# Linear attention of a macaron layer: the stage as a pipeline of 32 token tiles instead of a loop over batches

## What is computed

```python
    def step(carry, inp):
        mem, z = carry
        q_s, k_s, v_s = inp
        sq = jax.nn.elu(q_s) + 1.0
        att_mem = sq @ mem / (sq @ z)
        sk = jax.nn.elu(k_s) + 1.0
        mem = mem + jnp.einsum('bhlk,bhlv->bhkv', sk, v_s)
        z = z + sk.sum(axis=-2, keepdims=True).transpose(0, 1, 3, 2)
        att_dot = jax.nn.softmax(jnp.einsum('bhik,bhjk->bhij', q_s, k_s) * scale, axis=-1)
        att = att_dot @ v_s
        att = gate * att_mem + (1.0 - gate) * att
        return ((mem, z), att)
```

## Time and profile before

| what | value |
|---|---|
| time, median of 3 executions | 2392.57 us (2383.55, 2392.57, 2393.95) |
| the profiled execution | 2382.67 us, its span 2381.0 us |
| busy over the span: PE, DVE, ACT, POOL | 80%, 62%, 39%, 23% |
| attention stage, 844.4 to 1470.8 us | 626.4 us: PE 509.0, DVE 375.9, ACT 191.8, POOL 66.7 us busy |
| TensorE's mean granted clock, whole span and this stage | 0.90 and 0.86 of full speed |
| before it (feed-forward 1), behind it (feed-forward 2 and the last sum) | 844.4 and 910.2 us |

### The profile page before, as it was taken

One profiled execution on the slowest core, in us unless ns is written; L12 is line 12 of the kernel. 1 busy time (PEld: TensorE's weight loads), 2 busy tenths in 40 slices (PEclk: granted clock), 3 DMA queues, 4 the chain that ended last, 5 costly groups with the idle time before them and its releaser, 6 DMA issues. The chain is left out here.

```text
span 2381.0 us, 41513 instructions
## 1 busy us (share of the span) xinstructions
PE 1916.0 (80%) x12512; PEld 1065.6 (45%) x12513; DVE 1488.0 (62%) x3530; ACT 935.8 (39%) x1694; POOL 553.3 (23%) x640
## 2 busy tenths in 40 slices
PE   1899999998499958887888884599999998499940
PEld 1433333332299925565555663223333332189930
DVE  1678888884345437656666653487888886345533
ACT  0156666667222223332333321036666666322200
POOL 2222333311322231111001000222233331222246
PEclk9899999999699978888988986679999999799975
DMA  8336333320122231111011003335333330022245
GB/s 186 62 56 130 65 65 62 58 45 11 53 73 73 70 121 36 54 54 53 12 45 54 28 19 67 81 65 128 66 69 57 63 59 12 27 79 73 72 131 180
DMA packets 163076, 161.68 MB, mean 68 GB/s; under 512 B 20620, under 2 KB 153484, under 8 KB 162572
## 3 DMA queue, kind: packets, MB, share of 16 engines
q1 hardware_dynamic: 122048, 107.34, 19.7%
q10 hardware_dynamic: 30636, 27.21, 4.2%
q0 software_dynamic: 10240, 25.18, 3.7%
HBM read 90.80 MB, written 62.39 MB: 64 GB/s over the span
## 5 line engine op out<-in xcount | busy, mean ns | idle before, releaser
L576 DVE TENSOR_REDUCE f_M<-bank 128x1 f32<-128x512 f32 x1024 | 673.8, 685 | 194.0 <-PE bank L846 184.1
L486 ACT ACTIVATE f_PT<-bank 128x512 f32<-128x512 f32 x1024 | 573.0, 596 | 296.8 <-PE bank L863 292.2
L846 PE MATMUL bank<-f_KS,f_QS 96*128 96x512 bf16 x1024 | 403.8, 400 | 75.1 <-DVE f_M L576 39.1
L863 PE MATMUL bank<-f_QS,f_KS 99*128 99x512 bf16 x1024 | 394.8, 390 | 45.4 <-ACT f_PT L486 31.3
L863 PEld LDWEIGHTS bank<-f_QS,f_KS 99*128 99x128 bf16 x1024 | 99.9, 99 | 423.0 <-ACT f_PT L486 304.9
L873 PE MATMUL bank<-f_PT,f_V 128*32 128x512 f32 x2048 | 273.2, 607 | 0.0
L846 PEld LDWEIGHTS bank<-f_KS,f_QS 96*128 96x128 bf16 x1024 | 100.8, 99 | 204.8 <-DVE f_M L576 137.0
L1107 PE MATMUL bank<-f_room,f1m_gT 128*128 x568 | 136.2, 383 | 0.1
L1107 PE MATMUL bank<-f_room,f2m_gT 128*128 x568 | 135.3, 381 | 0.1
L415 POOL DMA_INDIRECT routed_rows<-f_AO,f_rows_i x128 | 124.7, 974 | 42.0 <-issue 42.0
L1107 PEld LDWEIGHTS bank<-f_room,f1m_gT 128*128 128x128 f32 x568 | 103.6, 193 | 11.8 <-issue 0.5
(11 more groups left out here) (257 smaller groups left out, 3027.4 us busy)
## 6 DMA issues: line engine op xcount, KB each, us to landing
f_QS<-q_parts SPq DMA_DIRECT2D x192, 64.0 KB
f_KS<-k_parts SPq DMA_DIRECT2D x168, 64.0 KB
expert_rows<-f1m_y ACTq DMA_DIRECT2D x71, 128.0 KB, 1.7
expert_rows<-f2m_y ACTq DMA_DIRECT2D x71, 128.0 KB, 1.7
xr<-f_xr SPq DMA_DIRECT2D x16, 512.0 KB, 3.0
f_room<-in_L_ffn_w SPq DMA_DIRECT2D x2, 4096.0 KB, 22.4
q_parts<-f_q SPq DMA_DIRECT2D x16, 384.0 KB, 2.5
k_parts<-f_k SPq DMA_DIRECT2D x16, 384.0 KB, 2.5
```

The source lines that it names most:

```text
L486: act.activation(PT[:, i % 8, :], SCE[i % 2][:, :], ACT.Exp).then_inc(probs_ready, 1)
L576: dve.tensor_reduce(M[:, t, h:h + 1], SCM[(a * SC + i) % 3][:, :], AX.X, ALU.max).then_inc(scm_drained, 1)
L846: pe.matmul(SCM[(a * SC + i) % 3][:, :], QS[par][0:K_MAX, h, t * P:(t + 1) * P], KS[par][0:K_MAX, h, :], start=True, stop=True).then_inc(s ...
L863: pe.matmul(SCE[i % 2][:, :], KS[par][0:K_EXP, h, t * P:(t + 1) * P], QS[par][0:K_EXP, h, :], start=True, stop=True).then_inc(sce_filled, 1)
```

## The change

It rewrites `attention_pass` and nothing else of weight. No arithmetic of the reference is left out.

- **One pipeline.** `SLOTS` becomes a list of 37 pairs (b, t), all written out, without a hardware loop: four slots that only prepare batch 0 (b = -1), 32 slots for the 32 tiles, and one behind them. Slot (b, t) holds score, recall, probabilities and from_memory of its tile g, and weigh, add_up, turn_out, project_out and put_out of tile g - 1.
- **Items.** `PLACES` gives the items of batch b + 1 to four places A to D in each of the four slots, k before q (`qk` 0 to 3 are now k). The last one, `mem` 6, falls into place A of the next batch's first slot. `sk` 0 waits for the four k features only, each `mem` item for its own v and sk, and `recall` for the memory of its own tile (`drained["mem"]` of 2t + 1) instead of the whole batch.
- **Banks.** Scores and recall share banks 0 and 1 (`SA`), so `recall` waits for `s_ready` of its tile and `score` for `am_read` of the tile before. `LB` is two banks, 2 and 3; `OB` is bank 4 and holds only `turn_out` and `project_out`. The ring has three banks, 5 to 7.
- **The sum.** `add_up` is (AM - L) * gate + L, three operations (two of them read PSUM) in place of gate * AM, omg * L and their sum (one of them reads PSUM). All three now stand between `weigh` and `turn_out`.
- **x** stays on chip in four buffers; x1, its store and its reload are gone, and `put_out` adds in place. Preparing batch b + 2 is cut into four parts, one for each slot. The steps for `gate` come behind the normalisation of batch 0.

```diff
+    PLACES = [{"A": [("hsT", 0), ("hsT", 1)], "B": [("qk", 0)], "C": [("qk", 1)], "D": [("qk", 2)]},
+              {"A": [("qk", 3), ("qk", 4)], "B": [("v", 0)], "C": [("v", 1)], "D": [("sk", 0)]},
+              {"A": [("mem", 0), ("mem", 1), ("qk", 5)], "B": [("sk", 1)], "C": [("qk", 6)], "D": [("v", 2), ("mem", 2)]},
+              {"A": [("qk", 7), ("mem", 3)], "B": [("sk", 2)], "C": [("v", 3), ("mem", 4)], "D": [("sk", 3), ("mem", 5)]}]
+    LATE = ("mem", U - 1)
...
-        SC, AMB, LB, OB, RING = bank[0:2], bank[2:4], bank[4], bank[5], bank[6:8]
+        SA, LB, OB, RING = bank[0:2], bank[2:4], bank[4], bank[5:8]
...
+            for a in range(1, XB):
+                load_x(a)
+            for b in range(B):
+                sp.wait_ge(y_ready, (b + 1) * T)
+                sp.dma_start(x_out[b].rearrange("(t p) d -> p t d", p=P), X[b % XB][:, :, :]).then_inc(y_stored, 16)
+                sp.wait_ge(y_stored, (b + 1) * 16)
+                if b + XB < B:
+                    load_x(b + XB)
```

ScalarE's slot:

```diff
+            def slot(b, t):
+                g, before = tile(b, t), tile(b, t - 1)
+                if g is not None:
+                    act.wait_ge(s_ready, g + 1)
+                    act.activation(SS[:, g % 2, :, :], SS[:, g % 2, :, :], ACT.Exp, scale=SCALE).then_inc(e_ready, 1)
+                if (b, t) != SLOTS[0]:
+                    exponentials(*((b, t - 1) if t else (b - 1, T - 1)), "D")
+                evacuate(b, t, "A")
+                evacuate(b, t, "B")
+                exponentials(b, t, "A")
+                if g is not None:
+                    for half in range(2):
+                        act.wait_ge(pbT_filled, g * 2 + half + 1)
+                        if half == 0:
+                            wait(act, l_filled, g)
+                        act.activation(PBT[:, half * PAIRS:(half + 1) * PAIRS, :].rearrange("p h i -> p (h i)"),
+                                       LB[half], ACT.Copy).then_inc(pbT_ready, 1)
+                exponentials(b, t, "B")
+                if before is not None:
+                    act.wait_ge(attT_filled, before + 1)
+                    wait(act, o_filled, before)
+                    act.activation(attT[:, :, :].rearrange("p c i -> p (c i)"), OB, ACT.Copy).then_inc(attT_ready, 1)
+                evacuate(b, t, "C")
+                exponentials(b, t, "C")
+                evacuate(b, t, "D")
+                if t == 2 and b + 2 < B:
+                    root(b + 2)
```

VectorE's `add_up` and slot:

```diff
+            def add_up(g):
+                dve.wait_ge(l_filled, g + 1)
+                dve.wait_ge(am_read, g + 1)
+                wait(dve, attT_filled, g)
+                own(dve.tensor_tensor(AT[:, :], AM[:, g % 2, :], LB[0], ALU.subtract))
+                own(dve.tensor_tensor(AT[:, :], AT[:, :], w["gate"][:, :], ALU.mult))
+                dve.tensor_tensor(AT[:, :], AT[:, :], LB[0], ALU.add).then_inc(at_ready, 1)
...
+            def slot(b, t):
+                g, before = tile(b, t), tile(b, t - 1)
+                last = ((b, t - 1) if t else (b - 1, T - 1)) if (b, t) != SLOTS[0] else None
+                if g is not None:
+                    subtract_maximum(g)
+                if last is not None:
+                    lows(*last, "D")
+                    memories(*last, "D")
+                if before is not None:
+                    add_up(before)
+                if last is not None:
+                    features(*last, "C")
+                memories(b, t, "A")
+                if g is not None:
+                    probabilities(g)
+                if last is not None:
+                    features(*last, "D")
+                lows(b, t, "A")
+                if g is not None:
+                    from_memory(g)
+                features(b, t, "A")
+                lows(b, t, "B")
+                if b + 2 < B:
+                    prepare_batch(b + 2, t)
+                features(b, t, "B")
+                lows(b, t, "C")
+                memories(b, t, "C")
+                if before is not None:
+                    put_out(before)
```

TensorE's slot:

```diff
+            def slot(b, t):
+                g, before = tile(b, t), tile(b, t - 1)
+                if g is not None:
+                    score(g)
+                if before is not None:
+                    weigh(before)
+                make(b, t, "A")
+                if g is not None:
+                    recall(g)
+                make(b, t, "B")
+                if g is not None:
+                    turn_probabilities(g)
+                if before is not None:
+                    turn_out(before)
+                make(b, t, "C")
+                if before is not None:
+                    project_out(before)
+                make(b, t, "D")
```

More of the change, by code:

```diff
@@ new lines, in exponentials @@
+            def exponentials(b, t, place):
+                for item in items(b, t, place):
+                    kind, i, n = item
+                    if kind == "qk":
+                        act.wait_ge(low_ready, count(*item))
+                        act.activation(low[:, i % 2, :], low[:, i % 2, :], ACT.Exp).then_inc(ex_ready, 1)
+            def slot(b, t):
[25 more added lines that the diff above has]
+                    root(b + 2)
@@ L1600, in _ @@
             dve.wait_ge(init, INIT)
             call_for_rows(0)
+            for part in range(4):
+                prepare_batch(0, part)
             dve.wait_ge(gate_exp, 1)
@@ L1607, in _ @@
             dve.wait_ge(gate_step, 2)
-            dve.tensor_scalar(w["omg"][:, :], w["gate"][:, :], -1.0, 1.0, ALU.mult, ALU.add).then_inc(gate_step, 1)
-            dve.wait_ge(gate_step, 3)
-            s = Steps(dve, dve_front, 0, FRONT)
-            for stage in (combine_rows, variance, normalise):
-                stage(0, s)
-            run_turns(dve, turn)
+            for b, t in SLOTS:
+                slot(b, t)
         @block.tensor
@@ new lines, in recall @@
+            def recall(g):
+                n, t = divmod(g, T)
+                pe.wait_ge(s_ready, g + 1)
+                if t == 0:
+                    pe.wait_ge(sqk_ready, (n + 1) * QK)
+                pe.wait_ge(drained["mem"], n * U + 2 * t + 1)
+                carry(SA[0])
+                for h in range(H):
+                    pair, one = h // 2, h % 2
+                    part = slice(one * DK, (one + 1) * DK)
+                    for half in range(2):
+                        seg = slice((2 * t + half) * LSEG, (2 * t + half + 1) * LSEG)
+                        last = pe.matmul(SA[one][half * LSEG:(half + 1) * LSEG, pair * VW:(pair + 1) * VW],
+                                         sqk[n % 2][part, pair, seg], MEM[n % 2][part, 2 * t + half, pair, :], start=True, stop=True)
+                last.then_inc(am_filled, 1)
@@ new lines, in turn_probabilities @@
+            def turn_probabilities(g):
+                pe.wait_ge(pb_ready, g + 1)
+                for half in range(2):
+                    if half == 0:
+                        wait(pe, at_ready, g)
+                    else:
+                        wait(pe, pbT_ready, g * 2)
+                    for i in range(PAIRS):
+                        last = pe.transpose(LB[half][:, i * P:(i + 1) * P], PB[g % 2][:, half * PAIRS + i, :], ident[:, :])
+                    last.then_inc(pbT_filled, 1)
@@ L1622, in turn_out, with weigh @@
+            def weigh(g):
+                pe.wait_ge(pbT_ready, (g + 1) * 2)
+                n, t = divmod(g, T)
+                for h in range(H):
+                    last = pe.matmul(LB[0][:, h * DK:(h + 1) * DK], PBT[:, (h % 2) * PAIRS + h // 2, :],
+                                     V[n % 2][:, t, h, 0:DK], start=True, stop=True)
+                last.then_inc(l_filled, 1)
             def turn_out(g):
                 pe.wait_ge(at_ready, g + 1)
+                wait(pe, y_ready, g)
@@ L1796, in macaron @@
         }
-        x1 = nc.dram_tensor("x1", (B, S, D), F32, kind="Internal").ap()
         x2 = nc.dram_tensor("x2", (B, S, D), F32, kind="Internal").ap()
```

470 lines of the change are left out of this document (179 added, 291 removed).

## The result

| | before | after |
|---|---|---|
| time, median | 2391.93 us (4 runs, 2383.55 to 2393.95) | 2298.62 us (4 runs, 2296.95 to 2301.32) |
| ratio, 95% interval | | 0.9617 [0.9593, 0.9642] |
| span of the profiled execution | 2381.0 us | 2295.2 us |
| attention stage | 626.3 us | 536.7 us |

A forecast was written before the change was run, and what follows sets the result against it. TensorE was taken as the bound, neither full nor at full clock. Seven turns -68.6, start -2 and end +5.3 us on the profiled 2382.67 gave 2317.4, and 5.5 more to the median 2323 us, range 2280 to 2358.

The forecast's parts named there:

- A turn without the clock: Four slots at 2.4 GHz: TensorE's 53.4 us of work plus waits, mostly for VectorE's probabilities, 58.7 us a turn.
- The clock: TensorE's lower clock behind two waits over a microsecond a turn: 2 x 1.8 = 3.6 us, making 62.3 us a turn.
- two of the signs: Signs of being right: seven turns of 60 to 65 us, and a granted clock of 0.92 to 0.95 in them.
- The rule behind the term: On TensorE, one wait of over a microsecond costs itself and about 1.8 us at 1.2 GHz behind it.
- rival 3: Waits spread over all slots, each with two that pull the clock down: 73.1 us a turn, 2403 us; chance 0.05.
- VectorE's price for PSUM: In add_up, two operations read PSUM instead of one: nothing charged, 0.72 us from start to start each.
- The end: Last turn, without items to fill waits: slots of 13 us, the last 9; 61 against 55.7, +5.3, within 0 and +10.
- The start: Until batch 0 is prepared: 1 us from gate steps off the path, 1 us from its preparation, -2 us together.
- the x loads: Three more load_x on SyncE's queue beside the first gather: nothing to 2 us, taken as nothing.
- The 5.5 us from the profiled execution to the median: Added to the sum of 2317.4 because the profiled execution of the old kernel was at the low end: 2323 us.
- Rival 1: TensorE runs through as waits overlap better, VectorE beginning slots early: 55 us a turn, 2272 us in all; chance 0.12.
- Rival 2: Costlier hand-overs, and ScalarE's lists or the ring holding something: 67 us a turn, 2361 us in all; chance 0.13.

The follow-up runs named there:

- Experiments 5 and 6: Changed kernel with one, or three, unused VectorE reductions of 0.72 us ahead of the probabilities in slot 3: 2306.81 us, 0.9668, and 2331.42 us, 0.9767.
- experiment 10: Changed kernel with its three further x loads waiting for the first gather: 2297.22 us, 0.9604.
- Experiments 8 and 11: Changed kernel with weigh into OB, lists reordered and later x loads: 2276.70 us, 0.9541; the same with mem 4 moved behind sk 3: 2269.35 us, 0.9494.
- experiment 3: Changed kernel with two ring banks instead of three: 2321.64 us, 0.9711.
- experiment 4: Changed kernel with the second half of the turned probabilities back in OB, shared with turn_out and project_out: 2366.95 us, 0.9898.
- 2 the loop: Old kernel with its hardware loop written out and nothing else changed: 2383.61 us, 0.9967.

## Why the prediction was right, and where it was off

**A turn without the clock: right, and in part by luck, since two small errors lie against each other.** Forecast were slots of 14.3, 14.2, 15.2 and 15.0 us, 58.7 in all; measured 14.1, 14.2, 15.3 and 14.9, 58.5. TensorE's work is 54.3 us and not 53.4; 0.4 of the difference is weigh, which takes 1.83 and not 1.73 from start to start behind score. The waits cost 4.2 and not 5.3: the one in slot 3 1.9 (forecast 2.2), slot 2 1.1 (1.2), slot 0 0.9 (1.3), slot 1 0.3 (0.6). The kind of each wait and its place are as forecast. VectorE, busy 46.1 of 58.5 us, is not the bound.

**The clock: the step that failed.** The prediction charged 1.8 us for each of two waits over 1 us in every turn, 3.6 a turn, 25 us in all. Measured is 1.7 in one turn of seven. The size was right, how often it is paid was wrong, and so were two of the signs that the prediction named: the turns took 54.8 to 60.2 us and not 60 to 65, at a granted clock of 1.00 and not 0.92 to 0.95. Of the 28.7 us that the turns gained beyond the forecast, 23.5 are this term. Another 3.7 are the first turn, 54.8 us long: its first slot has no tile before it, hence no weigh, turn_out and project_out, which the forecast of seven equal turns left out. The rule behind the term doesn't hold as it stands: its threshold of "over a microsecond" came from two waits of a turn that was full of others. In the trace of before, the product after 1.11 us of waiting ran slowly, but the wait followed two more, of 0.61 and 0.47 us, in the 6 us ahead of it. In the changed kernel TensorE worked for 13 us without a pause ahead of the wait of 1.71 us, and works for some 12 behind it. Experiments 5 and 6 show the same place paying in 1 (up to 3), 5 and 7 turns of seven as its wait grows from 1.7 to 2.4 us and by another 1.4. What decides at a given length is not settled, and that the neighbouring waits made the difference in the old kernel is not shown. The Trainium skill (TensorE: Matmul & The Clock Gate, "A second HAM failure mode: psum-queue depth-cycling") reports of a bf16 kernel that short idles between groups that cycle through PSUM banks make the clock oscillate. The turns here, in f32, have such groups and two such idles each, at a clock of 1.00 in six of seven; that oscillation doesn't show. Had it, rival 3 would have come out.

**VectorE's price for PSUM: right at nothing.** The three operations of `add_up` in the stage of the changed kernel; the number behind the busy us is the mean ns of one. L1540 and L1542 read PSUM (bank), L1541 doesn't, and all three take the same time:

```profile
L1541 DVE TENSOR_TENSOR la_AT<-la_AT,gate 128x512 f32<-128x512 f32 x32 | 22.1, 692 | 1.1
L1540 DVE TENSOR_TENSOR la_AT<-la_AM,bank 128x512 f32<-128x512 f32 x32 | 22.0, 688 | 5.5 <-PE bank L1679 5.1
L1542 DVE TENSOR_TENSOR la_AT<-la_AT,bank 128x512 f32<-128x512 f32 x32 | 22.0, 687 | 1.1
```

**The end: right in sign and mechanism, too small.** +9.1 against +5.3, inside its bounds of 0 and +10. Its slots take 12.9, 14.3, 12.8 and 14.3 us, where 13 was forecast, and the last 10.6 instead of 9. The waits for the probabilities are 3.5 and 3.9 us long, and project_out runs at full clock in one slot and at half in the next:

```profile
1324.21 1.97 PE L1672 MATMUL bank<-ident,la_PB 128*128 128x128 f32 x8 [3.46 <-DVE la_PB L1518]
...
1327.72 1.99 PE L1694 MATMUL bank<-la_o,la_attT 128*128 128x256 f32 x8 [0.69 <-ACT la_attT L1434]
...
1336.75 1.97 PE L1672 MATMUL bank<-ident,la_PB 128*128 128x128 f32 x8 [3.85 <-DVE la_PB L1518]
...
1340.26 3.78 PE L1694 MATMUL bank<-la_o,la_attT 128*128 128x256 f32 x8 [0.69 <-ACT la_attT L1434]
```

**The start: the sum right by luck, two of its parts not.** -1.5 against -2. Taking the gate steps off the path fits the 1 us forecast: the first stretch is 24.9 us before and 23.9 in experiment 10. But the x loads were set at nothing and cost 2.8 us (experiment 10), and preparing batch 0 gained 3.3 instead of 1.

**The 5.5 us from the profiled execution to the median** were too many: the profiled execution of the changed kernel lies 1.7 us below its median. With the turns taken as 58.5, the end as +9, the start as -1.5 and nothing for the clock, the sum would have been 2382.7 - 95.2 - 1.5 + 9 = 2295.0 for the profiled execution, which took 2296.95.

**The rivals.** Rival 1 named the size of what is possible, 55 us a turn, but gave the wrong reason: overlap alone doesn't reach it. Experiments 8 and 11 do, by another order. Rival 2 (more held by ScalarE and the ring, 67 us a turn) did not come; experiment 3, with one ring bank fewer, goes some way towards it with 62.0 us a turn. Where the gain comes from is then shown in part: experiment 4 gives the second bank for the turned probabilities 68 us, 3 the third ring bank 23, 2 the loop 7, while x on chip and recall by tile are each worth nothing that shows. These can't be summed to the 93, since each was undone alone and one wait can hide another. What the new order of the tiles gives by itself is not shown.

## What to carry to other kernels

When one engine is the bound, look at whose output it waits for and what stands ahead of that on the other engine's list: new orders on three engines, among them three operations moved behind the one that is waited for, gave 22 us together with a bank and later loads, where the bank alone gave nothing. Separate two uses of a PSUM bank early if one of them waits for a copy in every step: here that was worth 68 us. Charge a wait by how often its clock price is paid in the trace at hand, not as certain: here a wait of 1.71 us, with some 12 us of work on both sides of it, mostly cost no more than itself.

## What the runs showed that was not expected

- The same wait of 2.43 us is followed by products at 2.4 GHz in two turns and by 1.7 us of loss in the five others, with the same instructions around it.
- Three loads of 512 KB issued beside the first gather took SyncE 4.6 us to issue (1.5 us behind the gather), and the gathered rows landed 2.8 us later.
- The hardware loop of two passes cost 7 us, 3 us in each of two turns: TensorE stood 4.06 us between the passes and ran at the lower clock behind it.
- About half of what the turns gained, and more than half of what a missing ring bank took back, is TensorE's clock and not its waits (some 47 of 97 us, and 18.6 of 26.8).
